# Attention and feed-forward kernel: condition loaded as one row, mixing weights ahead of the square product, small products spread over the first stage

## What is computed

```
w[b]  = (weight / 16) * cond[b][None, :]        # 256 x 256, each column times one number
w[b]  = w[b] * rsqrt(sum(w[b]**2, axis=1) + 1e-8)
x    += tanh(reshape(w[b] @ C) @ W0 @ A1 @ A2 + bias)            # layer 0
Q1, K1 = cond @ Wq1 + bq1, cond @ Wk1 + bk1     # one row per batch
Q2, K2 = x @ Wq2 + bq2, x @ Wk2 + bk2
A     = softmax(Q2 K2' / 16) - alpha * softmax(Q1 K1' / 16)
x    += ffn(A @ ([cond, x] @ Wv + bv))          # int8-like rounding of activations and weights
```

## Time and profile before

| | |
|---|---|
| median of 3 runs | 240.14 us (239.92, 240.14, 242.85) |
| the profiled execution | 242.43 us |
| its span, first to last instruction | 240.5 us |
| PE busy, share of the span | 96% |
| DVE, ACT, POOL | 62%, 51%, 29% |
| mean granted clock of TensorE | 0.984 of full |

### The profile page before, as it was taken

How to read it: one execution, slowest core, us unless ns; L and a number is a source line. 1 busy time by engine, 2 the same in 40 slices (tenths; PEclk the granted TensorE clock), 3 DMA queues, 4 the chain that set the end, 5 groups by cost and what they waited for, 6 DMA issues and landing times.

```text
span 240.5 us, 3882 instructions
## 1 busy us (share of the span) xinstructions
PE 230.2 (96%) x1455; PEld 188.7 (78%) x1455; DVE 149.8 (62%) x325; ACT 121.9 (51%) x222; POOL 70.9 (29%) x97
## 2 busy tenths in 40 slices
PE   7987999999999999999999999999999899998994
PEld 7977899988997899989999899889999544433342
DVE  0744322887466557855886546546555597999963
ACT  2567603666324444345344434445435669944932
POOL 8340910444000000480663400000000065663850
PEclk9999968999999999999999999999999999999999
DMA  5990019000000000000000000000000000000044
GB/s 182 301 337 13 0 34 329 24 0 3 0 0 0 3 0 0 3 0 3 3 0 0 3 0 0 3 1 0 3 0 3 1 0 0 3 0 0 0 172 177
DMA packets 7105, 9.61 MB, mean 40 GB/s; under 512 B 800, under 2 KB 4912, under 8 KB 7088
## 3 DMA queue, kind: packets, MB, share of 16 engines
q1 hardware_dynamic: 6624, 9.11, 11.0%
q10 hardware_dynamic: 144, 0.26, 0.4%
q0 software_dynamic: 320, 0.01, 0.1%
HBM read 7.28 MB, written 2.10 MB: 39 GB/s over the span
## 4 chain that ended last, share of the span: by engine, by line
PE 81%; DVE 10%; issue 4%; ACT 2%; POOL 2%; POOLq 0%; DVEq 0%
PE ps L1017 54%; PE ps L1164 6%; DVE hmax L860 4%; PE ps L1347 3%; PE ps L1064 3%; PE ps L1001 2%; PE ps L1299 2%; DVE hid L855 2%; PE ps L1047 1%; PE ps L1204 1%; PE ps L1373 1%; PE ps L1009 1%; PE ps L1103 1%; POOL hid L980 1%; DVE hi L902 1%
## 5 line engine op out<-in xcount | busy, mean ns | idle before, releaser
L1017 PE MATMUL ps<-vh,pth 128*128 128x256 f32 x128 | 37.3, 292 | 0.3 <-DVE ptl L605 0.3
L1017 PE MATMUL ps<-vl,pth 128*128 128x256 f32 x128 | 36.1, 282 | 0.0
L1017 PE MATMUL ps<-vh,ptl 128*128 128x256 f32 x128 | 36.1, 282 | 0.0
L480 ACT ACTIVATE prob<-ps,small 128x1024 f32<-128x1024 f32 x16 | 17.8, 1115 | 21.7 <-DVE small L750 21.7
L495 ACT ACTIVATE outT<-ps,small 128x128 f32<-128x128 f32 x32 | 10.0, 366 | 33.7 <-PE ps L1204 33.7
L1017 PE MATMUL ps<-x1h,xh 128*128 128x512 f32 x64 | 26.2, 409 | 0.0
L748 DVE TENSOR_REDUCE small<-ps 128x1 f32<-128x1024 f32 x16 | 19.6, 1222 | 10.1 <-PE ps L1017 9.9
L1017 PE MATMUL ps<-x1h,xl 128*128 128x512 f32 x64 | 25.2, 393 | 0.0
L1017 PEld LDWEIGHTS ps<-vh,pth 128*128 128x128 f32 x128 | 24.4, 191 | 0.9 <-issue 0.9
L1017 PE MATMUL ps<-x1l,xh 128*128 128x512 f32 x64 | 25.0, 390 | 0.0
L1017 PEld LDWEIGHTS ps<-vl,pth 128*128 128x128 f32 x128 | 24.5, 191 | 0.0
(11 more groups left out here) (226 smaller groups left out, 557.2 us busy)
## 6 DMA issues: line engine op xcount, KB each, us to landing
result<-yst SPq DMA_DIRECT2D x8, 256.0 KB, 2.1
xn<-in_x SPq DMA_DIRECT2D x4, 256.0 KB, 5.9
xn<-in_x SPq DMA_DIRECT2D x2, 512.0 KB, 9.2
wdn<-in_L_ffn_w_down SPq DMA_DIRECT2D x1, 704.0 KB, 7.4
wgn<-in_L_ffn_w_gate SPq DMA_DIRECT2D x1, 640.0 KB, 4.4
wun<-in_L_ffn_w_up SPq DMA_DIRECT2D x1, 640.0 KB, 5.3
a<-in_L_ffn_aux_weight SPq DMA_DIRECT2D x2, 256.0 KB, 6.2
wvf<-in_L_cond_Wv SPq DMA_DIRECT2D x1, 512.0 KB, 10.8
```

Source lines behind the costliest of these rows:

```text
L480: act.activation(prob[:, j % 2, :], ps[:, 2 * (j % 2):2 * (j % 2) + 2, :], ACT.Exp, bias=col("nb", j % 2), scale=ATT_SCALE, accum_out=col( ...
L1017: last = pe.matmul(dst, a, b, start=(n == 0), stop=(n == len(passes) - 1))
```

## The change

1. cond is loaded as one row of 512 numbers on one partition (`yrow`). PE spreads it to 128 partitions with one product, a column of ones times the row, into bank 1, behind 18 idle transposes (`WARM0` is now 18); 20 idle transposes follow (`WARM1`), and 8 stand before the mixing weights (`WARM2`). DVE reads cond from PSUM and waits for `ybc_ps` in place of the transfer.
2. PE transposes `wmix` of batch 0 ahead of the square product A1'W0', and that of batch 1 behind `mix(0)`. ACT's and DVE's copies follow that order; ACT takes the high part of the first piece of x before it copies W0'.
3. The small rows are transposed into bank 3 early, and DVE copies `cols` behind the low part of batch 0.
4. The four groups of small products are spread: one before and one behind the square product G, one behind each half of `mix(2)`. The last half still raises `vec_ps`.

```diff
-    WARM0 = 34
-    WARM1 = 8
+    WARM0, WARM1, WARM2 = 18, 20, 8
...
-            act.dma_start(ybc[:], cond.partition_broadcast(P)).then_inc(ld_y, 16)
+            act.dma_start(yrow, cond.rearrange("b d -> (b d)").rearrange("(a n) -> a n", a=1)).then_inc(ld_y, 16)
...
             row_norms()
+            x0_hi(0)
             act.wait_ge(wfT_ps, 1)
             copy(wfT, blocks(7), wfT_ready)
-            x0_hi(0)
+            mixT_hi(0)
             act.wait_ge(dn_ready, 1)
...
-            mixT_hi(0)
-            mixT_hi(1)
             act.wait_ge(wa1T_ps, 1)
             copy(wa1T[:], blocks(2), wa1T_ready)
             x0_hi(1)
             mixed_hi(0)
+            mixT_hi(1)
...
-            dve.wait_ge(ld_y, 16)
+            dve.wait_ge(ybc_ps, 1)
             dve.wait_ge(ld_mix, 16)
             for k in range(B * DC):
-                dve.tensor_tensor(wmix[:, k // DC, k % DC, :], wl[:, k % DC, :], ybc[:, k // DC, :],
+                dve.tensor_tensor(wmix[:, k // DC, k % DC, :], wl[:, k % DC, :], blocks(1)[:, k // DC, :],
                                   ALU.mult).then_inc(v_ready, 1)
...
+            mixT_lo(0)
+            dve.wait_ge(rowsT_ps, 1)
+            dve.tensor_copy(cols[:], ps[:, 3, 0:16]).then_inc(cols_ready, 1)
...
             mixed_lo(0)
+            mixT_lo(1)
             dve.wait_ge(mh_ready, 1)
             low(flat(ml[:]), ps[:, 3, :], flat(mh[:]), ml_ready)
             mixed_lo(1)
-            dve.wait_ge(rowsT_ps, 1)
-            dve.tensor_copy(cols[:], ps[:, 6, 0:16]).then_inc(cols_ready, 1)
...
             pe.wait_ge(ident_ready, 1)
-            for _ in range(WARM0):
-                pe.transpose(ps[:, 0, 0:P], ident[:], ident[:])
+            def warm(n):
+                for _ in range(n):
+                    pe.transpose(ps[:, 0, 0:P], ident[:], ident[:])
+
+            warm(WARM0)
+            pe.wait_ge(ones_ready, 1)
+            pe.wait_ge(ld_y, 16)
+            pe.matmul(ps[:, 1, :], ones[0:1, :], yrow, start=True, stop=True).then_inc(ybc_ps, 1)
+            warm(WARM1)
             x_T(0)
             pe.wait_ge(ld_wf, 16)
             square_T(7, wf).then_inc(wfT_ps, 1)
-            for _ in range(WARM1):
-                pe.transpose(ps[:, 0, 0:P], ident[:], ident[:])
+            pe.wait_ge(ld_rows, 16 * 7)
+            pe.transpose(ps[:, 3, 0:16], rows[:], ident[0:16, 0:16]).then_inc(rowsT_ps, 1)
+            warm(WARM2)
+            pe.wait_ge(w_dve, DC)
+            square_T(6, wmix[:, 0]).then_inc(wT_ps, 1)
             pe.wait_ge(ld_a1, 16)
             pe.wait_ge(wfT_ready, 1)
             square_mm(2, a1, wfT).then_inc(wa1T_ps, 1)
-            pe.wait_ge(w_dve, DC)
-            square_T(6, wmix[:, 0]).then_inc(wT_ps, 1)
+            mix(0)
             pe.wait_ge(w_act, DC)
             square_T(7, wmix[:, 1]).then_inc(wT_ps, 1)
-            mix(0)
...
             mix(1)
-            pe.wait_ge(ld_rows, 16 * 7)
-            pe.transpose(ps[:, 6, 0:16], rows[:], ident[0:16, 0:16]).then_inc(rowsT_ps, 1)
             pe.wait_ge(ld_qk, 32)
-            pe.wait_ge(cols_ready, 1)
+            square_T(6, wq2s).then_inc(qkT_ps, 1)
             pe.wait_ge(wTl_ready, B)
-            square_T(6, wq2s).then_inc(qkT_ps, 1)
             square_T(7, wk2s).then_inc(qkT_ps, 1)
...
+            bias_vector(0, wkT, C_BQ2)
+            square_mm(6, wqT, wkT).then_inc(g_ps, 1)
+            bias_vector(2, wqT, C_BK2)
+            mix(2, {0: lambda: cond_vectors(4, wq1s), 1: lambda: cond_vectors(8, wk1s).then_inc(vec_ps, 1)})
```

More of the change, by code:

```diff
@@ L152, in build_block @@
         on_s = sb("on_s", [P, 2, D], F32)
-        ybc = on_s
+        yrow = on_s[0:1].rearrange("p a b -> p (a b)")
         tcol = sb("tcol", [P, NT], F32)
@@ L274, in build_block @@
         xh_ready, xl_dve, xl_pool = sem("xh_ready"), sem("xl_dve"), sem("xl_pool")
+        ybc_ps = sem("ybc_ps")
         wfT_ps, wfT_ready, wa1T_ps, wa1T_ready = sem("wfT_ps"), sem("wfT_ready"), sem("wa1T_ps"), sem("wa1T_ready")
@@ L636, in _, with mixT_lo @@
             low(xl[:, 0, 1, half(0)], xn[:, 0, 1, half(0)], xh[:, 0, 1, half(0)], xl_dve)
-            for b in range(B):
+            def mixT_lo(b):
                 dve.wait_ge(wTh_ready, b + 1)
                 low(flat(wTl[:, b]), ps[:, 6 + b, :], flat(wTh[:, b]), wTl_ready)
+            mixT_lo(0)
+            dve.wait_ge(rowsT_ps, 1)
+            dve.tensor_copy(cols[:], ps[:, 3, 0:16]).then_inc(cols_ready, 1)
             def mixed_lo(n):
@@ L1018, in three_passes, with mix @@
                 return last
-            def mix(n):
+            def mix(n, behind=None):
                 b, q0 = n // 2, 2 * (n % 2)
@@ L1034, in mix @@
                     last.then_inc(ct_ps, 1)
+                    if behind:
+                        if c == 0:
+                            pe.wait_ge(ld_q1, 32)
+                        behind[c]()
             def x_T(n):
@@ L1072, in _, with bias_vector @@
             square_mm(2, a1, wfT).then_inc(wa1T_ps, 1)
-            pe.wait_ge(w_dve, DC)
-            square_T(6, wmix[:, 0]).then_inc(wT_ps, 1)
+            mix(0)
             pe.wait_ge(w_act, DC)
             square_T(7, wmix[:, 1]).then_inc(wT_ps, 1)
-            mix(0)
             pe.wait_ge(wa1T_ready, 1)
             pe.wait_ge(ld_a2, 16)
+            pe.wait_ge(cols_ready, 1)
             square_mm(3, wa1T, a2).then_inc(m_ps, 1)
             mix(1)
-            pe.wait_ge(ld_rows, 16 * 7)
-            pe.transpose(ps[:, 6, 0:16], rows[:], ident[0:16, 0:16]).then_inc(rowsT_ps, 1)
             pe.wait_ge(ld_qk, 32)
-            pe.wait_ge(cols_ready, 1)
+            square_T(6, wq2s).then_inc(qkT_ps, 1)
             pe.wait_ge(wTl_ready, B)
-            square_T(6, wq2s).then_inc(qkT_ps, 1)
             square_T(7, wk2s).then_inc(qkT_ps, 1)
[L1089 to L1095, removed]
+            def bias_vector(at_col, wT, bias):
                 for m in range(DC):
@@ L1099, in _, with cond_vectors @@
                                   cols[:, bias + k:bias + k + 1], start=(k == 0), stop=(k == DC - 1))
-            for at_col, w in ((4, wq1s), (8, wk1s)):
+            def cond_vectors(at_col, w):
                 for m in range(DC):
@@ L1105, in _ @@
                                          stop=(k == DC - 1))
-            last.then_inc(vec_ps, 1)
-            mix(2)
+                return last
+            project(0)
+            pe.wait_ge(wqT_ready, 1)
+            pe.wait_ge(wkT_ready, 1)
+            bias_vector(0, wkT, C_BQ2)
+            square_mm(6, wqT, wkT).then_inc(g_ps, 1)
+            bias_vector(2, wqT, C_BK2)
+            mix(2, {0: lambda: cond_vectors(4, wq1s), 1: lambda: cond_vectors(8, wk1s).then_inc(vec_ps, 1)})
             pe.wait_ge(vec_ready, 4)
```

## The result

The changed kernel takes 242.16 us (median of 18 executions, 240.35 to 242.52), the kernel before 239.87 (18, 238.73 to 242.85). The ratio is **1.0065 [1.0039, 1.0091]**: slower by about 1.6 us. (The ratios here leave out executions more than 1.5% above the fastest of their kernel; the medians hold all.) Forecast were 238.7 us and 236.3 to 241.0. The profiled execution after took 242.39 us, its span 240.6, against 242.43 and 240.5 before: two single executions of one time, though 3.7 us less was expected.

The account below looks back on a forecast made before the run. PE, busy 96% of the span, was taken as the bound. Terms -3.30 + 1.07 - 1.73 + 0.45 - 0.2 = -3.7 us, off the profiled 242.43, gave 238.7 us; range 236.3 to 241.0.

Parts of the forecast that it names:

- Part 4, the head: Start of the kernel, cond's row and spreading product: `mix(0)` starts at 14.0 instead of 14.22, -0.2 us.
- rival 2: Start of the kernel: PE's pace rises late because of the one-partition product; 242.0 us, at worst 245.2; chance 0.10.
- Part 2: Small rows transposed early, between `mix(1)` and Wq2's transposes: wait and transpose leave the path, -1.73 us.
- Part 3: Mixing weights ahead of the square product: batch 1's four transposes come onto the path behind `mix(0)`, +0.45 us.
- Part 1: Small products spread around G and `mix(2)`: -3.30 us if the clock no longer falls, +1.07 for a new wait.
- rival 1: Around the spread small products: the clock falls all the same, elsewhere; price 1.7 to 3.3, 240.4 to 242.0 us; chance 0.25.
- Rival 3: Whole run: the median had paid the clock's fall in full, so all of -3.7 comes off, 236.4 us; chance 0.15.

Follow-up runs that it names:

- e10: The changed kernel with both groups of cond products behind the first half of `mix(2)`, so the second half covers DVE's steps: 239.38 us, 0.999.
- e3: The changed kernel with the spreading product over all 128 partitions, zeros under the row of cond: 240.09 us, 1.0033.
- e14: e10 with the spreading product over 128 partitions, as in e3: 237.98 us (6 executions), 0.9917.
- e5: e1 with four idle products of one partition and 128 columns in place of 8 of its 34 idle transposes: 240.19 us, 1.0011.
- e15: e13 with an idle product of one partition and 512 columns in place of 8 of its 34 idle transposes: 236.43 us (6 executions), 0.9867.
- e4: The changed kernel with all small products together again between the square product G and `mix(2)`: 239.18 us, 0.996.
- e9: e8 with ACT copying W0' before the high part of x again, and the small rows transposed behind the square product: 238.51 us, 0.9953.
- e16: The changed kernel with ten idle transposes on PE in the wait between the last small product and `vec_ready`: 239.45 us, 0.9985.
- e13: e9 with the small products placed as in e10: 236.75 us (6 executions), 0.9874.
- e12: The kernel of e4 run once more, in a series with the changed kernel and e10: 238.42 us, 0.9942.
- e8: e1 with the small products together as in e4: 239.91 us, 0.9999.
- e1: The changed kernel with cond loaded by transfer to 128 partitions again, no spreading product, 34 idle transposes in a row: 239.83 us, 1.0006.
- e6: e5 with its four idle products over all 128 partitions: 240.53 us, 1.0017.

## Why the forecast was wrong

- **Part 4, the head: -0.2 forecast, +1.66 found, outside its bounds of -1.1 to +0.4.** Two steps of it failed. (1) "The pace rises at about 7.4 us, behind the product": I took the moment from a kernel in which nothing but transposes ran, and moved it unchanged to one with a product on one partition in between. It came at 10.74: 1.5 us of the loss are the 20 transposes (3.87 for 2.4), 0.6 the product, which ended at 7.63 (18 transposes took 0.23 each, not 0.21, and it 2.00, not 1.73). That was rival 2, at 0.10, and in e10 it holds in more than half of the executions, read by the kinds of their times, which lie 1.3 and 2.8 us above the lowest where I had priced 3.3 (its addends come to 6.7, not 6.5). e3 and e14 show that over 128 partitions the rise isn't late; e5 and e15 that one partition alone doesn't make it so. (2) "From its start to the end of the scaled batch 0 it took 4.35": in the change it took 5.4 (7.66 to 13.08), since L628 collided with POOL. The edit of ACT's order stood in the diff, and I followed it on ACT alone and not to POOL, which waits for what ACT makes. In the change the late pace hid this one; where the rise is timely this chain of DVE is what PE waits for (e4: `mix(0)` at 14.57, not 14.0). e9 shows some 0.5 to 0.7 us for this and the next point together.
- **Part 2: -1.73 right, "costs nothing" wrong.** The wait of 1.38 is gone. But I didn't ask when the small rows land: 10.3 to 11.1 us, ahead of which PE rests 0.8 us in kernels with a timely rise.
- **Part 3: +0.45 right** (0.44).
- **Part 1, the step "If the clock no longer falls": the condition was false.** The wait's size (1.07) and its cause (DVE's L671 to L679) were right, and so was -3.30 locally (-3.19). The clock fell behind the wait: **rival 1**, by its own mechanism and price (1.60 against 1.7 at the least). A fall came in 60 of 78 executions of kernels with that rest. I gave it 0.25, and for reasons that the runs don't bear out: "`x_T(1)` follows directly" didn't help, and the 1.38 us of rest at 22 us had dense work on both sides, not thin products. The Trainium skill's rule on gaps ("TensorE: Matmul & The Clock Gate", section "Why this matters for your kernels"), which I had set aside because the fall before came without a gap, names the kind of cause that acted here: e16 filled the gap and e10 removed it, and no fall came in 24 executions. But the gaps that it warns of are longer than this one of 1.07 us: by its words this wait was no danger, and my reading of it in the prediction ("the new wait would be the danger") went further than they do. Nor does a gap alone say when a fall comes: thin products without one bring it too (the kernel before, 75 of 110; e9, 12 of 12).
- **The comparison with the median.** Rival 3 is out: the median paid 1.2 us of the fall, not all. I had seen that the profiled execution was of the dearer kind, and still weighed part 1 as if it were the change's largest gain. Against the executions without a fall (238.8) it had nothing to give, only 1.07 us to cost.

The terms as the medians have them: head +1.66, +0.44, -1.73, wait +1.07 and +0.26, falls 1.60 after against 1.2 before, +0.4: +2.1. The medians differ by 2.3, and the ratio gives 1.6 +- 0.6.

## What to carry to other kernels

Before a fall of the clock is charged to a stretch of thin work, sort the executions by their mean granted clock: what the median holds of it may be a third of what the profiled execution shows, and that third is all that a cure can give. Don't cure it with an order in which TensorE must wait for a small chain on VectorE; leave dense work between the last small product and the wait (e10, e13), or fill the rest (e16). And follow a reordered copy to everybody who waits for it: an engine that starts a microsecond earlier can shut out a tiny step on the critical path.

## What the runs showed that was not expected, and what stays open

- A product of 512 columns over **one partition** among the idle transposes at the start kept the granted clock from rising, in 4 of 7 profiled executions, over 128 partitions it did not (2 profiled): the 20 transposes behind it took 3.9 to 4.5 us against 2.35. PE rested in neither.
- The rise fell into two groups, 5.4 to 5.6 us and 10.35 us or later, in seven profiled executions with that product. What puts an execution into the one or the other is open, and so is why e5 and e15, idle products on one partition, hardly showed it; e15 has only six executions. A product of the row that DVE doesn't read wasn't tried.
- Small products in a row, the same order in all four, brought a fall in 7 of 24 executions behind the head with the row's product (e4, e12) and in 23 of 24 behind the one with the transfer (e8, e9). The falls in those 24 are why part 4 costs 2.7 us beside the one head and nothing beside the other. Why the head matters so much 15 us later is open.
- No fall followed a rest of 0.8 us at 10 us in e1 and e3, of 1.12 us there in e5, or of 1.38 us at 22 us in the kernel before. One followed 1.73 us in e6 (0.50 from 11.28 to 14.69), and 1.07 us behind 0.8 us of thin products in the change. What decides between them was not measured.
- A lighter transfer of cond let `wl` land in 2.7 us in place of 5.1:

```profile
wl<-in_L_cond_weight SPq DMA_DIRECT2D x1, 256.0 KB, 2.7
```

It was worth nothing, since DVE waited for PE's product until 7.66.
